# First attention of a decoder kernel: query norms added to the scores as a second diagonal product on TensorE

## What is computed

```
s     = einsum('bihd,bjhd->bhij', qr, conj(kr)).real          # scores, q and k rotated by phases
qn    = (q.real ** 2 + q.imag ** 2).sum(-1)                   # query norms, one per row i
kn    = (k.real ** 2 + k.imag ** 2).sum(-1)                   # key norms, one per column j
maha  = maximum(qn[i] + E*E * kn[j] - 2*E * s, 0) / V         # E = exp(-mu |i-j|), V depends on |i-j|
logits = coef * log1p(maha / nu) - 0.5 * DH * log(V)          # causal mask, then softmax over j
```

## Time and profile before

| what | value |
|---|---|
| median of 3 runs | 2977.43 us (2976.34 to 2983.90) |
| profiled execution, its own time | 2985.12 us |
| profiled execution, span from first to last instruction | 2983.4 us |
| mean granted TensorE clock | 0.837 |
| PE busy | 2374.3 us, 80% |
| DVE busy | 1791.3 us, 60% |
| ACT busy | 1069.6 us, 36% |
| POOL busy | 749.5 us, 25% |

### The profile page before, as it was taken

How to read it: one execution, slowest core, us unless ns; L and a number is a source line. 1 busy time by engine, 2 the same in 40 slices (tenths; PEclk the granted TensorE clock), 3 DMA queues, 4 the chain that set the end, 5 groups by cost and what they waited for, 6 DMA issues and landing times.

```text
span 2983.4 us, 42978 instructions
## 1 busy us (share of the span) xinstructions
PE 2374.3 (80%) x15312; PEld 1736.1 (58%) x15312; DVE 1791.3 (60%) x3970; ACT 1069.6 (36%) x2714; POOL 749.5 (25%) x637
## 2 busy tenths in 40 slices
PE   3977879786886969788796969878797878969588
PEld 2665647664565646665575636755476655756344
DVE  8965359534886249653795249753595337862554
ACT  2442225432342325423253324523253323533133
POOL 1541025300452005310362005410253004520000
PEclk8987879888887969878798978879798877879699
DMA  4000000000000000000000000000000000010000
GB/s 154 1 1 1 1 23 1 1 1 8 16 1 1 1 23 1 1 1 1 23 1 1 1 23 1 1 1 1 23 1 1 1 3 21 1 63 1 8 14 14
DMA packets 17235, 32.84 MB, mean 11 GB/s; under 512 B 2702, under 2 KB 8854, under 8 KB 16230
## 3 DMA queue, kind: packets, MB, share of 16 engines
q1 hardware_dynamic: 15718, 25.60, 2.5%
q0 software_dynamic: 1280, 4.20, 0.4%
HBM read 23.49 MB, written 5.77 MB: 10 GB/s over the span
## 4 chain that ended last, share of the span: by engine, by line
PE 48%; DVE 34%; issue 11%; ACT 5%; POOL 1%; DVEq 0%; SPq 0%; ACTq 0%; DMA 0%; POOLq 0%
PE bank L844 46%; DVE work L381 8%; DVE work L399 4%; DVE work L390 4%; DVE work L379 3%; ACT work L638 3%; PE bank L848 2%; DVE st L332 2%; DVE act_row L339 1%; DVE max L543 1%; DVE work L548 1%; ACT act_T L638 1%; DVE mv L335 1%; DVE negmax L401 1%; ACT ln_t L638 1%
## 5 line engine op out<-in xcount | busy, mean ns | idle before, releaser
L844 PEld LDWEIGHTS bank<-work 128*128 128x128 f32 (+1 forms) x4128 | 358.4, 215 | 167.9 <-issue 166.6
L844 PE MATMUL bank<-work 128*128 128x128 f32 (+1 forms) x4128 | 379.5, 307 | 64.0 <-DMA work<-in_wo 34.6
L638 ACT ACTIVATE work<-work 128x512 f32<-128x512 f32 (+1 forms) x456 | 271.5, 622 | 395.4 <-DVE work L444 149.8
L638 ACT ACTIVATE work<-bank 128x512 f32<-128x512 f32 x424 | 232.0, 593 | 408.3 <-PE bank L844 380.3
L381 DVE TENSOR_TENSOR work<-bank,table_space 64x512 f32<-64x512 f32 x512 | 352.1, 688 | 6.8
L844 PE MATMUL bank<-sb_cols,work 128*128 128x1 f32 x2048 | 271.7, 262 | 102.0 <-ACT work L638 102.0
L844 PEld LDWEIGHTS bank<-sb_cols,work 128*128 128x128 f32 x2048 | 268.0, 211 | 120.0 <-ACT work L638 119.7
L638 ACT ACTIVATE work<-bank,sb_b_up 128x512 f32<-128x512 f32 x288 | 198.0, 687 | 270.6 <-PE bank L844 265.4
L844 PEld LDWEIGHTS bank<-sb_w_down,work 128*128 128x128 f32 x2304 | 267.3, 192 | 30.6 <-issue 30.6
L519 DVE SCALAR_TENSOR_TENSOR work<-bank,wexp,work 128x128 f32<-128x128 f32 x256 | 72.1, 345 | 353.9 <-PE bank L844 353.9
L844 PE MATMUL bank<-act_T,sb_w_up 128*128 128x512 f32 x576 | 278.1, 631 | 0.0
(11 more groups left out here) (234 smaller groups left out, 3437.6 us busy)
## 6 DMA issues: line engine op xcount, KB each, us to landing
sb_w_up<-in_w_up SPq DMA_DIRECT2D x1, 2304.0 KB
sb_w_down<-in_w_down SPq DMA_DIRECT2D x1, 2304.0 KB
x_T<-in_x_T POOLq DMA_DIRECT2D x8, 256.0 KB, 2.9
x_row<-in_x_row POOLq DMA_DIRECT2D x8, 256.0 KB, 3.0
ctx_T<-in_ctx_T SPq DMA_DIRECT2D x8, 256.0 KB, 2.7
work<-in_ctx_row SPq DMA_DIRECT2D x8, 256.0 KB, 3.4
out<-act_row SPq DMA_DIRECT2D x8, 256.0 KB, 2.3
x_scratch<-act_row SPq DMA_DIRECT2D x7, 256.0 KB, 2.5
```

The costliest lines, as they stand in the source:

```text
L638: return nc.scalar.activation(o, i, f, **k)
L844: return nc.tensor.matmul(o, l, r, start=start, stop=stop, skip_group_check=True)
```

## The change

Before, DVE added the query norm term to the scores: four instructions per head computed `dec_inv * qn + scores` from the bank into a working tile, and a fifth one took the minimum with 0 and multiplied by the weight. In the changed kernel POOL builds a second diagonal matrix per head, from the query norms, into a new tile `diag_q` (two buffers). PE multiplies it with the table `dec_inv` (1/E) in four more 128x128 f32 products, which accumulate into the score bank. DVE's fifth instruction then reads the bank itself, and the four others are gone. PE waits for both diagonals before the first product of a head.

```diff
@@ vector, step s, head h = s - 2
                         M = rows(wk[(11, 21)[h % 2]])
-                        dve.wait_ge(norms_sb, g * H0 + h + 1)
                         dve.wait_ge(score, g * H0 + h + 1)
-                        for b in range(GB):
-                            last = v.scalar_tensor_tensor(M[:, b], dec_inv[:, h], nrm[:, h % 2, 4 + b:5 + b],
-                                                          rows(bank[4 + h % 2])[:, b], ALU.mult, ALU.add)
-                        link(last)
-                        v.scalar_tensor_tensor(M, M, 0.0, bc_h(wgt, h), ALU.min, ALU.mult).then_inc(maha, 1)
+                        v.scalar_tensor_tensor(M, rows(bank[4 + h % 2]), 0.0, bc_h(wgt, h), ALU.min,
+                                               ALU.mult).then_inc(maha, 1)
@@ gpsimd, step s, head h = s - 1
-                        q.tensor_tensor(rows(wk[(22, 10)[h % 2]]), ident[:].unsqueeze(1).broadcast_to([128, GB, N]),
-                                        nrm[:, h % 2, 0:4].unsqueeze(2).broadcast_to([128, GB, N]),
-                                        ALU.mult).then_inc(diag_done, 1)
+                        for half_norms, tile in ((slice(0, 4), diag_k[h % 2]), (slice(4, 8), diag_q[h % 2][:])):
+                            q.tensor_tensor(tile, ident[:].unsqueeze(1).broadcast_to([128, GB, N]),
+                                            nrm[:, h % 2, half_norms].unsqueeze(2).broadcast_to([128, GB, N]),
+                                            ALU.mult).then_inc(diag_done, 1)
@@ tensor, scores_of(h)
-                    pe.wait_ge(diag_done, g * H0 + h + 1)
+                    pe.wait_ge(diag_done, g * 2 * H0 + 2 * h + 2)
                     if h >= 2:
                         pe.wait_ge(maha, g * H0 + h - 1)
                     S = bank[4 + h % 2]
                     mm(S[:], dec[:, h], wk[(22, 10)[h % 2]][:], stop=False)
+                    for b in range(GB):
+                        mm(rows(S)[:, b], diag_q[h % 2][:, b], dec_inv[:, h], start=False, stop=False)
                     for b in range(GB):
```

More of the change, by code:

```diff
@@ L119, in decoder @@
         nrm = sb("nrm", 128, 2, 8)
+        diag_k = [rows(wk[22]), rows(wk[10])]
+        diag_q = [sb(f"diag_q{i}", 128, GB, N) for i in range(2)]
         negmax = sb("negmax", 128, 2, GB)
```

## The result

The changed kernel takes **3046.8 us** (3044.5 to 3051.1, 4 runs). The kernel before took 2980.7 us on the same chip (2976.3 to 3007.2, 4 runs). The ratio is 1.0205, with a 95% interval of 1.0143 to 1.0266: slower by 2%, and by 1.4 to 2.7% within the interval. The forecast was 3037, with a range of 3003 to 3090. The profiled execution took 3047.3 us, where the sum had come to 3044.

A forecast was written before the change was run, and what follows sets the result against it. PE and DVE were both taken as full in short steps, DVE bounding only while POOL disturbs it. Steps 7 to 15 +49, steps 2 to 6 -7, tail +17: +59 us on 2977.4, forecast 3037 us, range 3003 to 3090.

The forecast's parts named there:

- PE's added matmuls: PE, each head's step: four more 128x128 f32 products take 0.89 us, 0.111 us per record.
- The stall: PE, ahead of the diagonal product: waiting for POOL's second diagonal costs 0.72 us in every step; N is the norms' start.
- The step: PE, norms to norms of one head in the full loop: 7.48 + 0.89 + 0.72 = 9.09 us.
- the first row of the table: Steps 7 to 15 of the first attention, less one block of norms: 641 us against 592 over eight groups, +49 us.
- DVE idles, and the minimum stands at 0.69: Sign on DVE: about 2 us idle a step ahead of the rotation of q, minimum at 0.69 us everywhere.
- Steps 2 to 6: Early steps, PE lighter without output and at first values: 38.1 us a group against 39.0, -7 us over eight groups.
- The tail: Norms of step 15 to the residual add, one serial chain: 35.5 us a group, 284 against 267, +17 us.
- Term (a): Tail: norms of head 15 wait for squares behind the k sum, starting at N + 6.65 instead of 5.64, +1.0 us.
- term (c): Tail: the diagonals of head 15, on the path alone, add 1.0 us.
- term (d): Tail: the four added matmuls of head 15 at full clock add 0.9 us.
- The first rival: PE's clock falls within the steps, two falls a group adding 23 to 46 us; 3062 to 3130 us, chance 0.20.
- the nine steps: First attention, q projection of step 7 to end of step 15's norms: 80.1 us per group forecast, +49 over eight.

The follow-up runs named there:

- experiment 1: Changed kernel with the query-diagonal products issued after the q.k products, each product waiting only for its own diagonal: 2959.0 us, ratio 0.9952 to the kernel before.
- experiment 6: Changed kernel with one more, unused diagonal on POOL between the two, PE waiting for all three: 3180.7 us, ratio 1.0693 to the kernel before.
- experiment 3: Kernel before with both diagonals built on POOL and PE waiting for both, the second unused, DVE's work unchanged: 3034.6 us, ratio 1.0205.
- experiment 4: Kernel before with only DVE's relief: its four query-norm instructions dropped, the norms left out of the scores: 2848.2 us, ratio 0.9574.
- experiment 10: Changed kernel with query-diagonal products last for even heads, odd heads as in the kernel before: 2956.7 us, ratio 0.9926 to the kernel before.

## Why the prediction was right

- **PE's added matmuls**, +0.89 us a step: exact, 0.89 in the changed kernel and in experiments 1 and 6. The prediction took the 0.111 us per record of its row, and the row was right.
- **The stall.** Predicted: diagonal product at N + 4.23; measured: N + 4.22. That POOL's chain sets it is shown by experiment 6 (+1.00 for one more diagonal) and by experiment 1 (the stall goes, and with it 2.5% of the kernel).
- **The step**, 9.09 predicted, 9.20 measured. The arithmetic missed 0.11 us: the diagonal product behind the wait takes 523.83 - 522.86 = 0.97 us to the next instruction, where it takes 0.86 without a wait (122.33 - 121.47 in experiment 1). The same 0.97 stands behind the longer wait of experiment 6 (124.93 - 123.96). Over 72 steps 0.11 us is 7.9 us, which is the miss of the first row of the table (56.5 against 49). Two slips of the arithmetic changed nothing: the earlier trace rows give the diagonal 1.11 us, not 1.04, and 2977.4 + 59 is 3036, not 3037.
- **DVE idles, and the minimum stands at 0.69**: 2.13 and 0.49 us, predicted "about 2"; the minimum's mean is 692 ns.
- **Steps 2 to 6**: -7.6 against -7. Here errors offset each other. Steps 3 to 6 took 6.97, 6.97, 7.87 and 8.30 us, each 0.10 to 0.12 over the forecast, again the 0.11 above; step 2 took 7.9 us in the mean of the groups and not 8.4.
- **The tail**, 36.1 us a group and not 35.5. Term (a) was right: the norms of head 15 start at N + 6.62 (predicted 6.65). In groups 0, 2, 4 and 6 the whole tail takes 35.4 to 35.5 us, as forecast. In the other four it takes 36.4 to 36.9, since term (c) had a consequence that was not priced. Timeline of PE in the tail of group 7:

```profile
2654.44 1.84 PE L843 MATMUL bank<-sb_cols,work 128*128 128x1 f32 x16
2661.06 3.57 PE L843 MATMUL bank<-sb_cols,work 128*128 128x1 f32 x16 [4.78 <-ACT work L636]
...
2673.52 1.35 PE L843 MATMUL bank<-work,table_space 128*128 128x512 f32 x2 [2.46 <-POOL diag_q L802]
2674.67 1.91 PE L843 MATMUL bank<-table_space,diag_q 128*128 128x128 f32 x8
2676.38 1.69 PE L843 MATMUL bank<-work 128*128 128x128 f32 x8
```

And in the tail of group 6:

```profile
2324.54 1.12 PE L843 MATMUL bank<-work,table_space 128*128 128x512 f32 x2 [2.46 <-POOL diag_q L802]
2325.50 1.05 PE L843 MATMUL bank<-table_space,diag_q 128*128 128x128 f32 x8
2326.39 1.06 PE L843 MATMUL bank<-work 128*128 128x128 f32 x8
```

Behind the wait of 2.46 us for the diagonals of head 15 the clock falls a second time in group 7: the products with `diag_q` take 2676.38 - 2674.67 = 1.71 us, twice the 0.89 of term (d), which group 6 shows behind the same wait. The forecast had only one fall in the tail, ahead of head 14. Four such falls, at 1.3 us in the mean, are 5.2 us, which is the miss of 288.9 against 284.

- **The clock in the steps.** The first rival did not come. One view, busy time and granted clock by stretch (length; busy us of PE, PEld, DVE, ACT, POOL; clock; DMA share, GB/s), group 7, the nine steps and the tail, after:

```profile
2573.38:2654.44 81.06, 76.04 (x508) 59.98 (x508) 57.38 (x89) 40.56 (x125) 49.81 (x45) 1.00 0.00 1
2654.44:2690.79 36.35, 28.14 (x191) 25.56 (x190) 6.65 (x14) 15.54 (x51) 13.39 (x13) 0.81 0.00 1
```

And before:

```profile
2523.17:2597.08 73.91, 71.40 (x436) 54.93 (x436) 71.44 (x125) 40.38 (x125) 45.22 (x36) 0.93 0.00 1
2597.08:2629.97 32.89, 26.14 (x175) 23.76 (x174) 11.08 (x27) 15.68 (x51) 11.41 (x11) 0.84 0.00 1
```

The clock in the nine steps went up, from 0.93 to 1.00, and the waits of 1.25 us ahead of the norms are gone. It is not the relief alone that does this: experiment 3 relieves DVE of nothing and has a clock of 1.00 in the nine steps of all eight groups. In the tail of this group the clock went down, from 0.84 to 0.81; in the four groups without a second fall it is 0.86.

- **Everything outside**, taken as 0, came at -8. Other kernels show the same scatter, and no cause was sought.
- **Too little in one place.** The sum treated DVE's relief as if it had no other form. Against a kernel of gapless 7.48 us steps (experiment 4) the change costs 9.20 - 7.48 = 1.72 us in each of 72 steps, 124 us; it came out at +56.5 only because the same nine steps of the kernel before stood 67 us above the gapless 7.48 a step (592.0 against 524.8). Only 25 of these 67 us are idle time of PE. The other 42 are PE's own instructions, which last longer: group 7 has 71.40 us of them in the row above, where 65.6 is a gapless group, at a clock of 0.93. The prediction called the mean of 8.4 us a mixture of steps of 7.48 and 9.00 us; it is also one of two clock levels.

## What to carry to other kernels

When two engines are each full to within a few hundredths of a us, work moved from one to the other makes the second the bound; relief that was worth 4.3% alone was worth under 1% once its price stood on the other engine. Before an operation is moved, follow what its new inputs need: here the second POOL instruction and the wait for it, with DVE as loaded as before, cost 2.0%, and the matmuls alone 0.9%. Issuing last the products that need the late operand took the wait away. And ask first why the full engine is full: one operand moved from SBUF to PSUM gave 2.1% and two gave 3.0%, and no instruction was removed. Last, compare stage by stage: the total came within 3 us of the sum here, while the stage was off by 11.

## What the runs showed of the hardware

- Contention works both ways. DVE's instructions with two SBUF inputs go from 0.69 and 0.74 us to 1.23 and 1.75 beside POOL, and POOL's from 1.04 to 1.49 and from 1.26 to 1.72 (experiment 3).
- A matmul group of 0.86 us took 0.97 when it came behind a wait of 0.56 to 1.56 us, with the clock at its upper level on both sides.
- The granted clock fell behind one wait of 0.66 us ahead of the one-column norms and not behind another (experiment 10), and behind a wait of 2.46 us ahead of the diagonal product it fell in four groups and held in the four others (tail of the changed kernel). It held behind 1.56 us ahead of the diagonal product in the nine steps of every group in experiment 6. So the length of the wait alone does not tell it, and what does was not tested.
